# Expert products moved beside the output projection, with the denominators' small steps moved along

## What is computed

```python
xn = layernorm(x)
q, k, v = xn @ Wq, xn @ Wk, xn @ Wv                 # 16 heads of 64
attn = softmax(q k^T * 64**-0.5)                    # 2048 x 2048 per head
a = (attn v) @ Wo + bo
e = argmax(softmax(xn @ router_w^T))                # one of 8 experts
f = square(relu(xn @ expert_fc[e])) @ expert_proj[e]^T
return x + a + f
```

## Time and profile before

| | us |
|---|---|
| median of 3 runs | 1347.23 (1341.31 to 1350.61) |
| profiled execution, time | 1347.2 |
| its span, first to last instruction | 1345.5 |
| PE busy | 1324.2 (98%) |
| DVE busy | 1192.6 (89%) |
| POOL busy | 1121.0 (83%) |
| ACT busy | 708.4 (53%) |
| mean granted TensorE clock | 0.991 |

### The profile page before, as it was taken

How to read it: one execution, slowest core, us unless ns; L and a number is a source line. 1 busy time by engine, 2 the same in 40 slices (tenths; PEclk the granted TensorE clock), 3 DMA queues, 4 the chain that set the end, 5 groups by cost and what they waited for, 6 DMA issues and landing times.

```text
span 1345.5 us, 20239 instructions
## 1 busy us (share of the span) xinstructions
PE 1324.2 (98%) x6268; PEld 865.6 (64%) x6268; DVE 1192.6 (89%) x1890; ACT 708.4 (53%) x1230; POOL 1121.0 (83%) x884
## 2 busy tenths in 40 slices
PE   6899999999999999999999999999999999999998
PEld 3656667666676666776666776666766667765554
DVE  6888998998988999889988889889899889989997
ACT  4454566444465444565444664445654446654453
POOL 6689989777987778977788887879878789888997
PEclk8899999999999999999999999999999999999999
DMA  4222311333213321224112341124321234011101
GB/s 125 70 63 75 101 36 36 80 75 75 52 28 87 78 65 51 55 61 103 49 43 58 78 98 35 42 57 101 75 52 34 52 91 98 11 37 36 40 17 40
DMA packets 85867, 82.76 MB, mean 62 GB/s; under 512 B 24512, under 2 KB 54912, under 8 KB 85760
## 3 DMA queue, kind: packets, MB, share of 16 engines
q1 hardware_dynamic: 84736, 79.38, 23.7%
q0 software_dynamic: 1024, 2.10, 0.5%
HBM read 27.00 MB, written 6.29 MB: 25 GB/s over the span
## 4 chain that ended last, share of the span: by engine, by line
PE 96%; DVE 3%; issue 1%; DMA 0%; ACT 0%; POOL 0%; SPq 0%; DVEq 0%; POOLq 0%
PE OB L1184 33%; PE SB L1129 17%; PE SB L1136 17%; PE MB L1155 16%; PE XB L1212 2%; PE XB L1222 2%; PE XB L1110 2%; PE XB L1117 2%; DVE mx L787 1%; PE XB L1191 1%; PE XB L1192 1%; PE XB L1193 1%; PE MB L1169 0%; DVE mx L793 0%; PE OB L1092 0%
## 5 line engine op out<-in xcount | busy, mean ns | idle before, releaser
L539 POOL TENSOR_TENSOR acc<-acc,ex 128x512 f32<-128x512 f32 x691 | 911.6, 1345 | 29.6 <-ACT ex L663 1.5
L787 DVE TENSOR_REDUCE mx<-MB 128x1 f32<-128x512 f32 x992 | 639.8, 681 | 64.8 <-PE MB L1155 64.6
L663 ACT ACTIVATE ex<-SB 128x512 f32<-128x512 f32 x1024 | 608.4, 598 | 96.3 <-PE SB L1136 31.4
L1184 PE MATMUL OB<-ex,V 128*64 128x512 f32 x2048 | 447.2, 594 | 0.0
L1129 PE MATMUL SB<-Q,K 128*128 128x512 f32 x1024 | 411.3, 402 | 0.7 <-DVE mx L793 0.5
L1136 PE MATMUL SB<-Q,K 128*128 128x512 f32 x1024 | 400.4, 391 | 0.1
L1155 PE MATMUL MB<-K,Q 128*128 128x512 f32 x992 | 390.5, 394 | 1.4 <-DVE mx L787 1.1
L1184 PEld LDWEIGHTS OB<-ex,V 128*64 128x64 f32 x2048 | 144.1, 137 | 277.6 <-issue 274.0
L823 DVE TENSOR_TENSOR acc<-acc,ex 128x512 f32<-128x512 f32 x205 | 290.6, 1417 | 21.1 <-POOL acc L539 1.8
L693 ACT ACTIVATE osb<-OB 128x512 f32<-128x512 f32 x32 | 19.1, 597 | 449.1 <-PE OB L1184 449.1
L1129 PEld LDWEIGHTS SB<-Q,K 128*128 128x128 f32 x1024 | 193.2, 189 | 67.0 <-issue 27.6
(11 more groups left out here) (135 smaller groups left out, 636.2 us busy)
## 6 DMA issues: line engine op xcount, KB each, us to landing
Q<-high SPq DMA_DIRECT2D x124, 128.0 KB, 2.4
K<-high SPq DMA_DIRECT2D x112, 128.0 KB, 2.3
Q<-low SPq DMA_DIRECT2D x64, 128.0 KB, 2.3
rd<-rows_rd SPq DMA_DIRECT2D x62, 128.0 KB, 2.9
K<-low SPq DMA_DIRECT2D x56, 128.0 KB, 2.3
w<-fc SPq DMA_DIRECT2D x23, 256.0 KB, 2.8
w<-projT SPq DMA_DIRECT2D x23, 256.0 KB, 3.1
sorted_x<-res SPq DMA_DIRECT2D x1, 1472.0 KB, 7.0
```

The costliest lines, as they stand in the source:

```text
L539: pool.tensor_tensor(a[:, :], src[:, :], EX[h][kt][:, :], ALU.add).then_inc(done, 1)
L663: act.activation(EX[h][kt][:, :], SB[bank_of(n, 2 * kt + h)][:, :], ACT.Exp).then_inc(a_e[h], 1)
L787: dve.tensor_reduce(mx[:, m % 2, u:u + 1], MB[bank_of(m, i)][:, :], AX.X, ALU.max).then_inc(v_m, 1)
L1184: mm = pe.matmul(OB[own[h], :], V[:, k, own[h]], EX[h][k][:, :], start=(k == 0), stop=(k == NT - 1))
```

## The change

1. `expert_up` and `expert_down` leave the score phase. In block n PE now does, after the last score: `project(n - 1)`, `expert_down` of tile n - 5, `expert_up` of tile n - 4, V stage. They write two MB banks in place of XB, and wait for DVE's maxima of units 29 and 30. A tile's up product stands at the end of block r + 4 and its down product at the end of block r + 5, so up runs in blocks 4 to 26, down in 5 to 27. ACT's two copies follow the last exponential, POOL's `square` is at kt 2 of the next block.
2. The two weights have a load and a semaphore each, issued in the block in whose end they are used. On SP `load_tokens` now stands behind the second `spread_k`, and `store_tile` at the end of the list.
3. `sum_parts`, all four steps, is done in the V stage right behind `fold_sums` where the block is not in `LATE`. After a block of `LATE` it is done in the next block at kt 3, 5, 7 and 9 (before: kt 2 to 5), and POOL normalises ahead of kt 8 (before: 6).
4. `SORT` starts in block 0 (four scatters at kt 8 to 14), then six in block 1 and six in block 2; block 3 has none, leaves `LATE`, and gives one addition back to POOL. The first half is staged in block 0, the second in block 1. `FETCH` is 5, 6, 5 gathers in blocks 28, 29, 30 (before 6, 6, 4).

```diff
-AT_UP, AT_DOWN = 4, 10
-TILE0 = 5
-SORT = [(1, kt) for kt in (2, 4, 6, 8, 10, 12)] + [(2, kt) for kt in (2, 4, 13, 14)] + [(3, kt) for kt in (2, 4, 6, 8, 10, 12)]
-FETCH = [(n, kt) for n in (NB - 4, NB - 3) for kt in (2, 4, 6, 8, 10, 12)] + [(NB - 2, kt) for kt in (2, 4, 6, 8)]
-LATE = (0, 1, 2, 3, NB - 4, NB - 3)
+TILE0 = 4
+SORT = [(0, kt) for kt in (8, 10, 12, 14)] + [(1, kt) for kt in (2, 4, 6, 8, 13, 14)] + [(2, kt) for kt in (2, 4, 6, 8, 10, 12)]
+FETCH = [(NB - 4, kt) for kt in (5, 7, 9, 11, 13)] + [(NB - 3, kt) for kt in (2, 4, 6, 8, 10, 12)] + [(NB - 2, kt) for kt in (2, 4, 6, 8, 10)]
+LATE = (0, 1, 2, NB - 4, NB - 3)
...
+                def load_w1(r):
+                    wait(sp, t_up, r.times(1))
+                    sp.dma_start(w1[:, :], fc[expert(r), :, :].rearrange("e d h -> d (e h)")).then_inc(d_up, 16)
+                def load_w2(r):
+                    wait(sp, t_down, r.times(1))
+                    sp.dma_start(w2[:, :, :], projT[expert(r), :, :].rearrange("e (c p) d -> p (e c) d", p=P)).then_inc(d_down, 16)
...
-                        if kt == AT_ON and not (n.i is None and n.off == 0):
+                        if n.off and kt == (8 if n.off - 1 in LATE else 6):
                             normalise(n - 1)
...
                         if 0 < n.off < NB - 1:
-                            late = n.off - 1 in LATE
-                            if late and kt == 1:
-                                fold_sums(n - 1, 1)
-                            sum_parts(n - 1, kt - late)
+                            if n.off - 1 in LATE:
+                                if kt == 1:
+                                    fold_sums(n - 1, 1)
+                                if kt % 2:
+                                    sum_parts(n - 1, kt // 2)
...
                         if n.off not in LATE:
                             fold_sums(n, 1)
-                        if n.off == NB - 2:
                             for part in range(1, 5):
                                 sum_parts(n, part)
...
+                def expert_down(r, n):
+                    wait(pe, v_m, (n + 2).times(UNITS, -2))
+                    wait(pe, d_down, r.times(16, 16))
                     wait(pe, g_hid, r.times(1, 1))
                     for c in range(NC):
-                        mm = pe.matmul(XB[:, 0:D], hid[:, c * P:(c + 1) * P], w2[:, c, :], start=(c == 0), stop=(c == NC - 1))
+                        mm = pe.matmul(down_bank(n)[:, 0:D], hid[:, c * P:(c + 1) * P], w2[:, c, :],
+                                       start=(c == 0), stop=(c == NC - 1))
                     mm.then_inc(t_down, 1)
...
                         if not start:
                             project(n - 1)
+                        for r in tile_down(n):
+                            expert_down(r, n)
+                        for r in tile_up(n):
+                            expert_up(r, n)
                         times_v(n, 0, NT)
```

More of the change, by code:

```diff
@@ L247, in on_dve @@
                 return {t: [t] for t in range(1, NT)}
-            first = 11 if n.off == 0 else 9 if n.off in (1, 2, 3, NB - 4, NB - 3, NB - 2) else 10
+            first = 11 if n.off == 0 else 9 if n.off in (1, 2, NB - 4, NB - 3, NB - 2) else 10
             return {NT: list(range(first, NT))}
@@ L334, in under, with tile_up, tile_down, down_bank @@
             return a.unsqueeze(1).to_broadcast([P, n, a.shape[1]])
-        def has_tile(n):
-            return TILE0 <= n.off < TILE0 + TILES
+        def tile_up(n):
+            return [n - TILE0] if TILE0 <= n.off < TILE0 + TILES else []
+        def tile_down(n):
+            return tile_up(n - 1)
+        def down_bank(n):
+            return MB[bank_of(n + 1, UNITS - 3)]
+        def up_bank(n):
+            return MB[bank_of(n + 1, UNITS - 2)]
         with nc.Block() as block:
@@ L499, in one @@
                             spread_k(*job[1:])
-                    if n.off == 2:
+                    for r in tile_up(n + 1):
+                        load_tokens(r)
+                    for r in tile_up(n):
+                        load_w1(r)
+                    for r in tile_down(n):
+                        load_w2(r)
+                    if n.off == 1:
                         load_sort(1)
@@ L503, in one @@
                         load_wo(pair + 1)
[L504 to L509, removed]
                     if n.off < NB - 1:
@@ L513, in one @@
                         spread_q(n + 2)
+                    for r in tile_down(n):
+                        store_tile(r)
                 def last():
@@ L632, in one @@
                     for kt in range(1, NT):
-                        if kt == AT_ON and not (n.i is None and n.off == 0):
+                        if n.off and kt == (8 if n.off - 1 in LATE else 6):
                             normalise(n - 1)
-                        if kt == AT_UP + 1 and has_tile(n):
-                            square(n - TILE0)
+                        if kt == 2:
+                            for r in tile_down(n):
+                                square(r)
                         if on_pool(n, kt):
@@ L727, in rectify @@
                     wait(act, t_up, r.times(1, 1))
-                    act.activation(up[:, :], XB[:, :], ACT.Relu).then_inc(a_up, 1)
+                    act.activation(up[:, :], up_bank(r + TILE0)[:, :], ACT.Relu).then_inc(a_up, 1)
                 def take_result(r):
@@ L775, in one @@
                             high_q(n + 2)
+                    for r in tile_down(n):
+                        take_result(r)
+                    for r in tile_up(n):
+                        rectify(r)
                     if n.off < NB - 1:
@@ L1151, in max_unit @@
                         pe.wait_ge(v_m, UNITS - 2)
+                    for r in tile_down(m - 2) if i == 0 else ():
+                        wait(pe, a_res, r.times(1, 1))
+                    for r in tile_up(m - 2) if i == 1 else ():
+                        wait(pe, a_up, r.times(1, 1))
                     if i == 0 and (m.i is not None or m.off):
```

49 lines of the change are left out of this document (17 added, 32 removed).

## The result

The kernel after took 1409.91 us (median of 4 runs, 1404.39 to 1414.79), beside 1344.27 for the kernel before on the same chip: a ratio of 1.0484, with a 95% interval from 1.0447 to 1.0521. The forecast was 1357, within 1%, in a range of 1346 to 1365. It was wrong, by 53 us.

What follows compares the result with a forecast made beforehand. PE was taken to bound the kernel (96% of the chain). The terms -3.0 + 0 + 7.0 - 0.6 + 1.2 + 1.9 - 0.5 + 3.2 + 0.8 gave +10.0 on 1345.5, with 1.7 around it: 1357 us, range 1346 to 1365.

Steps and rivals of the forecast that it cites:

- Step 1: Up and down products beside Wo in 23 tiles: 0.13 us gained a tile, -3.0 us (0 to -3.9).
- Step 2: DVE's V stage in tile blocks, with four small steps of 1.6 us added: cost taken as 0.
- The ring: The three MB banks, which let PE go on about as long as DVE's list ends late (0.6 us) with n % 4 = 3.
- Step 3: Small steps behind LATE blocks: -1.0 us in each of blocks 1, 2, 3, 29, 30; together -0.6 outside blocks 1 and 2.
- rival of the overflow: DVE's V stage list ends too late and PE loses time in 23 blocks: +10 to +14, 1367 or more; chance 0.09.
- Step 4: Blocks 1 and 2: ACT's copy at kt 12 waits for the late key chunk and PE stops: +3.5 us each, +7.0.
- rival without the stop: No stop in blocks 1 and 2; POOL's wait there instead, +1.3 us for both: 1347.5 us; chance 0.12.
- step 7: TensorE's clock falls after PE's stops in blocks 1 and 2: +3.2 us (0 to 3.2); blocks 29 and 30: +0.8.
- the 28.5 given as a sign: Sign that the forecast is right: a score phase of blocks 1 and 2 of about 28.5 us, before 24.98.
- Step 5: POOL normalises ahead of kt 8, so Wo waits in blocks 29 and 30: +1.2 and +1.9 us; last block -0.5.
- half a fall: Clock loss taken for the two waits of 2 and 3 us in blocks 29 and 30: +0.8 us (0 to 3.2).
- Step 6: First scatters, four on POOL in block 0 (4.6 us): cost 0, up to +1 us.

Runs made afterwards that it cites:

- e12: Kernel after with V products at kt 1, 2, 6, 8, low_w at kt 5, and small steps, POOL's multiplication and gathers as before: 1347.5 us.
- e7: e2 with SP spreading the key chunk of kt 6 before it stores and spreads the reciprocal in blocks 1 and 2: 1350.05 us.
- e9: e7 with the scatters and gathers of kt 5 to 7 put behind POOL's normalise (SORT and FETCH alone changed): 1350.08 us.
- e2: Kernel after with low_w moved to the V stage of the same block, behind the four small steps: 1363.99 us.
- e1: Kernel after with AT_LOW taken back from kt 9 to kt 5: 1363.46 us.
- e5: Kernel after with POOL's additions in pairs, head 0 twice then head 1 twice, for kt 2 to 9 in blocks with n % 4 = 0: 1367.54 us.
- e3: Kernel before with AT_LOW changed from kt 5 to kt 9 and nothing else: 1397.79 us.

## Why the prediction was wrong

**The step that failed is the list of the change itself.** The prediction costs five places of the diff and not the line with `AT_LOW`. That line moves one DVE instruction by four kt. Its eight executions are 8.8 us of DVE's 1192.6, the sum gave the move nothing, and it made some 43.5 of the +57.8. In its place the runs showed a wait: `low_w` was shut out for 9.35 us beside POOL's additions, and PE stood still for 8.16. Would the rows have given the price? Not fully: in before the instruction took at most 1.36 us and nothing in the page says 9.4. What they did give is a sign, an addition of DVE beside POOL at 1.55 us. The Trainium skill ("GPSIMD Engine Reference", Specifications) says that GpSimd shares its SBUF interfaces with VectorE, and that DVE instructions with two SBUF inputs contend; the runs agree (0.41 us with one input against 9.35 with two). Contention as a price per instruction would have been 1 us here, though. That it can be a wait for the end of a stream was shown by the runs only.

**Step 1, the products.** The mechanism was right. PE of after in block 9, the eight passes of Wo, down and up:

```profile
460.77 1.05 PE L1244 MATMUL XB<-wo,osb 128*128 128x128 f32 x8
461.66 1.06 PE L1134 MATMUL MB<-w,up 128*128 128x128 f32 x8
462.55 1.06 PE L1126 MATMUL MB<-tokT,w 128*128 128x128 f32 x8
463.54 2.80 PE L1206 MATMUL OB<-ex,V 128*64 128x512 f32 x12
```

From 460.77 to 463.54 are 2.77 us, the 2.8 of the prediction. A block with n % 4 = 1 or 2 takes 40.59 (before 40.71 to 40.74): -0.12 to -0.15 where -0.13 was forecast. The -3.0 beside the row of the table is for all 23 tiles; its 18 blocks at -0.13 make -2.3, and measured are -1.8: -1.6 from twelve such blocks, -0.3 from the five with n % 4 = 3 (39.23, before 39.29) and +0.1 from block 16.

**Step 2, DVE's V stage.** It holds except behind n % 4 = 3, where the list was forecast 0.6 late and covered. The first maximum of block 8 was at 384.78, with the V stage's end at 382.83: 1.95 behind it, where 0.6 on the 1.0 of before makes 1.6. The ring did not cover it all, and blocks with n % 4 = 0 lost 0.15. The same happens where a V stage has few products ahead of it: behind block 3, block 4 took 43.09 (before 41.07, and the first up product is 0.9 of it), and behind block 27, block 28 took 42.05 (41.07). In block 4 of after PE waits for DVE:

```profile
222.84 0.50 PE L1177 MATMUL MB<-K,Q 128*128 128x512 f32 x1 [0.70 <-DVE mx L802]
```

Step 3 gave +0.3 for the one and didn't name the other: about 1 us each. In e12, with the small steps back in the score phase, blocks 4, 8 and 28 take 41.96, 42.85 and 41.07, so it is these steps. Block 3 gained 0.57 where 0.8 to 1.0 was forecast. The rival of the overflow thus came true at its weak places only, by under 3 us and not by 10.

**Step 4, the key chunk.** Right in mechanism, place and most signs: wait of `high` 5.37 (forecast 4 to 5), PE idle 4.20 (4). e7 shows the cause, SP's order: 10.1 us of blocks 1 and 2 go with it. The 1.0 us that they keep above before is near the +1.3 that the rival without the stop had from POOL's multiplication. The term was +5.1 a block with the clock and measured 6.1 and 6.6. In block 1 the chunk's last DMA went out 5.9 later, not 5.5, and so landed 40.0 us behind the V stage's start, not 39.1; from there to Wo it was 4.96 (3.3 + 1.6 = 4.9). In block 2 the clock took more (step 7). The score phase of block 1 was 31.1 us; the 28.5 given as a sign had left out the prediction's own 1.6 for the clock.

**Step 5, POOL's normalise.** Right: +1.5 and +2.1 for 29 and 30 (forecast +1.2 and +1.9), and e9 shows the cause. The chain of after shows PE's waits as `issue`, ahead of Wo:

```profile
1308.12 1.76 issue
1309.88 1.13 PE XB L1244 x8
...
1347.58 2.41 issue
1349.99 1.13 PE XB L1244 x8
```

**Step 7, the clock.** After 4.20 us of idle PE in block 1 the granted clock was 0.57 over 4 us, so 3.95 x 0.43 = 1.7 us (forecast 1.6). In block 2, after 4.19 us, it was 0.50 from 161.50 to 167.40, which makes 3.0: together 4.7 and not 3.2. Behind the 8.16 us of block 8 it cost 2.7. The waits of 1.8 and 2.4 us cost little beyond themselves: Wo's eight passes took 1.13 instead of 0.89, the V stage behind them its usual 13.88, and the granted clock stayed 1.00 from 1308 to 1316 and from 1348 to 1356. The trace agrees with the Trainium skill's rule ("TensorE: Matmul & The Clock Gate", § HAM oscillation) for the six long gaps; for the two short ones half a fall (+0.8) was too much.

**Step 6** cost nothing that shows: block 0 ended 2 us earlier, but kernels with the same block 0 differ by as much (74.98 in e7, 79.53 in e9, 73.47 in e2), and the clock that the program is granted in its first 75 us differs with them.

Without the missed line the forecast's mechanisms stand, its size less so: e1 and e2, the change with `low_w` out of harm's way, took 1363.5 and 1364.0, inside the range at its upper end, but 17.5 and 18 above the kernel before measured beside them, where +10 was forecast. From the V stage of block 0 to that of block 30, e1 is 16.5 us longer than before, by the forecast 10.5. The 6 us are terms above: 2.5 in blocks 1 and 2, 2.0 in blocks 3 and 4, 1.2 in the row of the tile blocks and 0.6 in blocks 8, 12, 20 and 24, less 0.3 in blocks 29 and 30.

## What to carry to other kernels

Read a diff by its constants first, and give each changed number a line in the sum, even the one that moves a single short instruction. Where DVE works on two SBUF tensors, look at what POOL does then: beside a run of POOL additions that alternate between two sums it can be shut out to the end of the run, and if PE waits for DVE every engine stands. Keep such an instruction out of that stretch, give it one input, or order POOL's additions in pairs. And before a small step is put later, look at what SP has queued behind it.

## What the runs showed of the hardware

- A DVE `tensor_tensor` of 128x256 with two SBUF inputs took 0.35 us in the V stage with POOL idle (e2) and 6.5 to 13.1 us when held, 16 times in four kernels. A hold passes over several POOL instructions and from `add` through `normalise` into the next `add`.
- It ended with POOL's last addition that doesn't depend on the one directly before. That dependence is what lets DVE in was tested by e5 alone. The ends of the 16 holds fit, and so do DVE's own additions in the V stage (`add_own`, two SBUF inputs): beside POOL's additions for one head, each of which needs the one before, none of the some 200 in each profile took over 2.5 us.
- What decides whether a hold begins stays open. At kt 3 to 8 one of 36 such instructions was held, at kt 9 and later 15 of 22 (e5 and block 0 left out). The one in block 16 of after, beside the same additions, took 0.79 us, though it, too, started 0.47 us ahead of POOL's next addition, as those held in blocks 8, 12, 20 and 24 did:

```profile
749.92 0.79 DVE L848 TENSOR_TENSOR wlo<-wraw,whi 128x256 fp32r<-128x256 f32 x1
```

- The four runs of e3 lie at 1388 to 1405, wider than the 1340 to 1351 of before's. One hold more in the slower runs, some 9 us, could do that; only the fastest run has a trace, so it isn't shown.
